# Decoder with a spiking delta-rule attention: chunk read on crossed quarters, sums of beta and alpha moved within the round

## The reference

```python
def step(carry, inp):
    s, mem = carry
    qt, kt, vt, sdt, abt, bbt = inp
    mem = DECAY * mem + sdt
    hard = (mem > THR).astype(x.dtype)          # the spike's value in the forward pass
    mem = mem - spike * THR
    alpha = jax.nn.sigmoid(abt + alpha_spike * spike)
    beta = jax.nn.sigmoid(bbt[..., None] + jnp.sum(spike * beta_spike, axis=-1, keepdims=True))
    active = (jnp.sum(hard, axis=-1, keepdims=True) > 0)
    alpha = jnp.where(active > 0, alpha, jnp.ones_like(alpha))
    beta = beta * active
    s = s * alpha[..., None]
    u = jnp.einsum('bhd,bhdv->bhv', kt, s)
    s = s - beta[..., None] * jnp.einsum('bhd,bhv->bhdv', kt, u)
    s = s + beta[..., None] * jnp.einsum('bhd,bhv->bhdv', kt, vt)
    out = jnp.einsum('bhdv,bhd->bhv', s, qt)
    return ((s, mem), out)
```

## Time and profile before

| | us |
|---|---|
| median of 3 runs | 1092.09 |
| lowest and highest | 1091.55, 1096.4 |
| profiled execution | 1096.75 |
| its span | 1095.0 |
| TensorE busy | 972.4 (89%) |
| VectorE busy | 698.6 (64%) |
| ScalarE busy | 482.7 (44%) |
| GpSimd busy | 208.7 (19%) |
| mean granted TensorE clock | 0.964 |

### The profile page before, as it was taken

One profiled execution on the slowest core, in us unless ns is written; L12 is line 12 of the kernel. 1 busy time (PEld: TensorE's weight loads), 2 busy tenths in 40 slices (PEclk: granted clock), 3 DMA queues, 4 the chain that ended last, 5 costly groups with the idle time before them and its releaser, 6 DMA issues. The chain is left out here.

```text
span 1095.0 us, 40049 instructions
## 1 busy us (share of the span) xinstructions
PE 972.4 (89%) x16722; PEld 648.9 (59%) x16722; DVE 698.6 (64%) x2514; ACT 482.7 (44%) x1378; POOL 208.7 (19%) x394
## 2 busy tenths in 40 slices
PE   7878768999998999999999888679999999999996
PEld 2333247777777777777777777446446546546542
DVE  2887886989889888898877765145424524714710
ACT  7667412555555555545555555313323423423311
POOL 7100201122122121221221220221210310310300
PEclk8999956999999999999999999889999999999999
DMA  3000000000000000000000000211000000100100
GB/s 97 0 1 1 1 1 3 4 4 4 4 4 4 4 4 4 4 4 4 4 5 11 22 4 4 96 37 27 7 1 21 24 1 15 27 1 3 31 1 10
DMA packets 18652, 13.83 MB, mean 13 GB/s; under 512 B 2491, under 2 KB 17259, under 8 KB 18475
## 3 DMA queue, kind: packets, MB, share of 16 engines
q1 hardware_dynamic: 18475, 11.28, 3.5%
HBM read 7.70 MB, written 1.05 MB: 8 GB/s over the span
## 5 line engine op out<-in xcount | busy, mean ns | idle before, releaser
L935 PE MATMUL banks<-work 64*64 64x64 f32 x3072 | 97.9, 234 | 24.9 <-DVE gates L674 12.9
L994 PE MATMUL banks<-work 64*64 64x32 f32 x2560 | 107.6, 224 | 5.8 <-ACT work L1351 5.0
L1285 ACT COPY work<-banks 128x128 f32<-128x128 f32 x160 | 42.8, 268 | 157.8 <-PE banks L970 157.7
L199 DVE SCALAR_TENSOR_TENSOR gates<-mom,gates 128x16 f32<-128x16 f32 x512 | 101.1, 197 | 9.5 <-ACT gates L1258 4.5
L203 DVE SCALAR_TENSOR_TENSOR mom<-gates 128x16 f32<-128x16 f32 x512 | 102.9, 201 | 5.0
L994 PEld LDWEIGHTS banks<-work 64*64 64x64 f32 x2560 | 92.5, 139 | 18.1 <-issue 10.0
L637 DVE COPY_PREDICATED gates<-work,banks 128x256 f32<-128x256 uint32 x192 | 101.9, 531 | 1.1
L935 PEld LDWEIGHTS banks<-work 64*64 64x64 f32 x3072 | 73.0, 139 | 43.2 <-issue 20.5
L531 POOL TENSOR_TENSOR mom<-mom 128x4 f32<-128x4 f32 x32 | 7.2, 223 | 384.4 <-ACT work L1330 384.4
L608 DVE TENSOR_TENSOR work<-work 128x256 f32<-128x256 f32 x160 | 67.8, 424 | 19.3 <-PE banks L935 18.7
L647 DVE TENSOR_TENSOR work<-work,banks 128x128 f32<-128x128 f32 x160 | 45.6, 285 | 48.4 <-PE banks L994 45.4
(11 more groups left out here) (263 smaller groups left out, 2140.8 us busy)
## 6 DMA issues: line engine op xcount, KB each, us to landing
work<-gates SPq DMA_DIRECT2D x28, 38.5 KB
qT<-in_x_dram SPq DMA_DIRECT2D x4, 256.0 KB, 3.8
work<-in_x_dram SPq DMA_DIRECT2D x4, 256.0 KB, 2.9
out_dram<-work SPq DMA_DIRECT2D x4, 256.0 KB, 2.3
gates<-in_w_ff_dram SPq DMA_DIRECT2D x3, 256.0 KB, 3.2
wv_sb<-in_wv_dram SPq DMA_DIRECT2D x1, 512.0 KB, 4.6
work<-in_w_out_dram SPq DMA_DIRECT2D x1, 512.0 KB, 4.0
gates<-in_x_Wq_dram SPq DMA_DIRECT2D x1, 512.0 KB, 5.0
```

The costliest lines, as they stand in the source:

```text
L199: ve.scalar_tensor_tensor(mem[:, :, t], neg_mem, -0.9, mem[:, :, t], ALU.mult, ALU.add).then_inc(charged, 1)
L935: last = pe.matmul(level_out(l)[to, a], KS[rows, n.two, hp], late[rows, hp], start=True, stop=True)
L994: last = pe.matmul(packed(psXT, l)[rows, a], Z[rows, l - 1, z], second_half(XT[:, n.two], l)[rows, a], start=True, stop=True)
L1285: ac.copy(first_half(Z[:, l - 1], l), packed(psZX_half, l)).then_inc(z_ok, 1)
```

## The change

The chunk read's outputs and the two halves of the state read swap partition halves (`to_out`), so that the chunk read uses crossed quarters; the tail's `front_out` reads the heads accordingly. The first three of the eight read products stand among the fifth XT products, the others at the round's end (`read_heads`, which has the three waits of `read_chunk` at each call). For gates from HP + 2 on (`early`), the alpha sums move from step 4 to step 2, `drive` from VectorE's step 4 to 2, and the sigmoid from ScalarE's step 5 to 3. The beta sums, their sigmoid and `beta` move from steps 1 and 2 of the following round to the end of the same round. The turn of KS moves from step 2 to 1. In step 4 of VectorE the query's scaling and two scan operations stand ahead of the add of XT. `prefixed` is the count of `kq_ok` for this: the last prefix counts one more where the next round's scaling precedes it.

```diff
--- before.py
+++ after.py
@@ -333,6 +333,9 @@
                 return by_chunk(counts(g))
             return counts(g).rearrange("p a (x t) -> p a x t", x=2)
 
+        def early(g):
+            return g.n > HP + 1
+
         def by_chunk_as(g, t):
             return t if g.n <= HP else t.rearrange("p (a x) t -> p a x t", x=2)
 
@@ -347,6 +350,9 @@
 
         def to_time(par, hp):
             return head_rows[hp // 2], 2 * par + hp % 2
+
+        def to_out(par, hp):
+            return head_rows[1 - hp // 2], 2 * par + hp % 2
 
         def at_level(par, hp):
             return head_rows[hp // 2], 2 * par + (hp // 2 + hp) % 2
@@ -381,6 +387,10 @@
 
         def by_chunk(t):
             return t.rearrange("p (b t) -> p b t", b=B)
+
+        def prefixed(n, l):
+            early = l == LEVELS - 1 and n.it + 1 < ROUNDS
+            return n.it * NKQ + l + 1 + early
 
         GATES = NC * HP
         QUARTER = C // HP
@@ -595,7 +605,7 @@
 
                 def prefix(n, l):
                     ve.wait_ge(lvl_mm, n.it * LEVELS + l + 1)
-                    ve.wait_ge(kq_ok, n.it * NKQ + l + 1)
+                    ve.wait_ge(kq_ok, prefixed(n, l))
                     if l == 0:
                         second = KQ[:, n.four].rearrange("p x a (j s) -> p x a j s", s=2)[:, :, :, :, 1]
                         by = aT[:, :, n.tok].rearrange("p a (j s) -> p a j s", s=2)[:, :, :, 0].unsqueeze(1)\
@@ -706,28 +716,33 @@
                         if l == 5 and gate:
                             alpha(gate)
                         spike(scan, h + 1)
+                        if l == 4 and aft2:
+                            scale_query(aft2)
+                        if l == 4:
+                            spike(scan, h + 2)
+                            spike(scan, h + 3)
                         if nxt:
                             add_xt(nxt, l)
-                        if l == 4 and gate:
+                        if gate and l == (2 if early(gate) else 4):
                             drive(gate)
-                        spike(scan, h + 2)
+                        spike(scan, h + (4 if l == 4 else 2))
                         if aft:
                             prefix(aft, l)
-                        spike(scan, h + 3)
+                        spike(scan, h + (5 if l == 4 else 3))
                         if aft:
                             suffix(aft, l)
-                        spike(scan, h + 4)
+                        if l != 4:
+                            spike(scan, h + 4)
                         if aft:
                             keep(aft, l)
-                        spike(scan, h + 5)
+                        if l != 4:
+                            spike(scan, h + 5)
                         if l == 1 and gate:
                             spikes(gate)
-                        if l == 2 and gate_old:
+                        if l == 2 and ramp == 0:
                             beta(gate_old)
                         if l == 3 and aft2:
                             scale_key(aft2)
-                        if l == 4 and aft2:
-                            scale_query(aft2)
                     spike(scan, 6 * NINV)
                     if cur:
                         update(cur, 0)
@@ -735,6 +750,8 @@
                     if aft2:
                         prefix(aft2, 0)
                         suffix(aft2, 0)
+                    if gate:
+                        beta(gate)
                     spike(scan, 6 * NINV + 1)
                     if aft2:
                         diagonal(aft2)
@@ -909,7 +926,7 @@
                 def level(n, l, gate=None, gate_old=None):
                     if l == 5 and gate:
                         pe.wait_ge(alpha_ok, gate.n + 1)
-                    if l == 3 and gate_old:
+                    if l == 1 and gate_old and gate_old.n >= HP:
                         pe.wait_ge(beta_ok, gate_old.n + 1)
                     if n.it == 0 and l == 0:
                         pe.wait_ge(zeroed, NZERO)
@@ -917,7 +934,7 @@
                         pe.wait_ge(folded, NFOLD)
                         pe.wait_ge(sd_ok, NSD)
                         pe.wait_ge(qk_ok, NQK)
-                    pe.wait_ge(kq_ok, n.it * NKQ + l + 1)
+                    pe.wait_ge(kq_ok, prefixed(n, l))
                     if l == 0:
                         pe.wait_ge(keys_ok, n.it + 1)
                     else:
@@ -981,19 +998,22 @@
                                          first_half(Z[:, l - 1], l)[rows, z], start=True, stop=True)
                     last.then_inc(x_mm, 1)
 
-                def make_xt(n, l, gate, gate_old):
+                def make_xt(n, l, gate, gate_old, cur=None):
                     if l == 1 and gate_old:
                         pe.wait_ge(be0_ok, gate_old.n + 1)
-                    if l == 5 and gate:
+                    if gate and l == (3 if early(gate) else 5):
                         pe.wait_ge(zal_ok, gate.n + 1)
                     pe.wait_ge(z_ok, n.it * NINV + l)
                     if n.it or l >= 2:
                         pe.wait_ge(xt_ok, n.it * NINV + l - 1)
-                    for head in straight:
+                    for i, head in enumerate(straight):
                         (rows, a), (_, z) = at_xt(*head), at_z(*head)
                         last = pe.matmul(packed(psXT, l)[rows, a], Z[rows, l - 1, z],
                                          second_half(XT[:, n.two], l)[rows, a], start=True, stop=True)
-                    last.then_inc(xt_mm, 1)
+                        if i == len(straight) - 1:
+                            last.then_inc(xt_mm, 1)
+                        elif l == NINV and cur and i % 2:
+                            read_heads(cur, halves[i // 2:i // 2 + 1])
 
                 def values(n):
                     pe.wait_ge(s_ok, n.it * 2)
@@ -1030,7 +1050,7 @@
                     for s in range(2):
                         for par in range(2):
                             hp = 2 * ((par + swap) % 2) + s
-                            (rows, hp), (to, a) = from_head(par, hp), to_time(par, hp)
+                            (rows, hp), (to, a) = from_head(par, hp), to_out(par, hp)
                             last = pe.matmul(o_out[to, a], KQ[rows, n.four, 1, hp], state[rows, n.b, hp, :],
                                              start=s == 0 and not swap, stop=False, skip_group_check=True)
                     last.then_inc(o_old if swap else o_half, 1)
@@ -1043,13 +1063,17 @@
                     pe.wait_ge(spk_ok, g.n + 1)
                     pe.matmul(counts(g), bdones[:, :], counts_as(g, spk[:, g.two]), start=True, stop=True).then_inc(count_mm, 1)
 
-                def spike_sums(g):
-                    pe.wait_ge(spk_ok, g.n + 1)
+                def spike_sums(g, nxt=None):
                     if g.n == 0:
                         pe.wait_ge(au_ok, NPAIR)
                         pe.wait_ge(padded, 2)
-                    if g.n:
-                        pe.wait_ge(beta_ok, g.n)
+                    if early(g):
+                        pe.wait_ge(be0_ok, g.n)
+                        pe.wait_ge(xt_ok, nxt.it * NINV + 1)
+                    else:
+                        pe.wait_ge(spk_ok, g.n + 1)
+                        if g.n:
+                            pe.wait_ge(beta_ok, g.n)
                     pe.matmul(psG[:, 0:B * C], wad_sb[:, g.hp, :], g.tokens(auT_all), start=True, stop=True)\
                         .then_inc(ab_mm, 1)
 
@@ -1064,15 +1088,16 @@
                     pe.matmul(psG[:, 0:B * C], bspike_bd[:, g.hp, :], spk[:, g.two],
                               start=False, stop=True, skip_group_check=True).then_inc(beta_mm, 1)
 
-                def read_chunk(n):
+                def read_heads(n, heads):
                     pe.wait_ge(e_ok, (n.it + 1) * LEVELS)
                     pe.wait_ge(o_old, n.it + 1)
                     pe.wait_ge(u_ok, n.it + 1)
-                    for head in halves:
-                        (rows, o), (_, a), (_, q) = to_time(*head), at_level(*head), at_x(*head)
-                        last = pe.matmul(o_out[rows, o], EA[rows, n.three, LEVELS, a], U[rows, q, :],
+                    for head in heads:
+                        (to, o), (rows, a), (_, q) = to_out(*head), at_level(*head), at_x(*head)
+                        last = pe.matmul(o_out[to, o], EA[rows, n.three, LEVELS, a], U[rows, q, :],
                                          start=False, stop=True, skip_group_check=True)
-                    last.then_inc(o_mm, 1)
+                    if heads[-1] == halves[-1]:
+                        last.then_inc(o_mm, 1)
 
                 def write_state(n):
                     pe.wait_ge(ksn_ok, n.it + 1)
@@ -1099,10 +1124,12 @@
                             spread_norm(3, l - 1)
                         if nxt:
                             make_z(nxt, l)
-                        if l == 1 and gate_old:
-                            beta_sums(gate_old, cur)
```

(40 more changed lines are left out.)

## The result

The changed kernel takes 1111.65 us (median of 4 runs, 1106.95 to 1117.86) against 1093.42 for the kernel before on the same chip: ratio 1.0144, 95% interval 1.0106 to 1.0183. Forecast were 1087.5 us and a range up to 1096; the time has the other sign and lies outside. The profiled execution took 1117.86 us (span 1116.1, before 1095.0).

A forecast was written before the change was run, and what follows sets the result against it. Neither TensorE (92% busy) nor VectorE (87%) was full, so their waits for each other bound the kernel. Gains 7.2+0.8+0.6 less losses 3.3 and 0.8 gave 4.5 us, taken off the 1092.09 median: about 1087.5, range 1077 to 1096.

The forecast's parts named there:

- Alpha sums in step 2: Sums on TensorE cost nothing under cover; drive replaces beta in VectorE's step 2, cost 0.06 us, level 3 at 10.08.
- Round's end: First state read's last product stays 0.85 us behind level 4, now 14.64; level 5 at 16.2, round 16.49 against 16.85.
- Step 4: Between levels 3 and 4, the alpha sums leave, 0.74 us less; level 4 at 13.78 us instead of 13.96.
- Beta at the round's end: Beta sums ahead of the read, and beta ahead of level 0's copy, put level 1 at 5.08 against 4.48: 0.60 lost.
- Read on crossed quarters: Fifth XT, held by the second state read and three inserted read products, ends 0.5 us later, bounds 0.2 to 0.9.
- rival 2: Slower: inserted read products hold the XT products behind them, 0.33 us in each of 30 rounds; time 1096, chance 0.11.
- VectorE's order in step 4: The query's scaling goes into VectorE's 0.80 us of idleness; alpha ends at 15.8 us instead of 16.51.
- Late rounds and the low clock: Rounds 25 to 30 lose 0.55 us each to held-up XT, 3.3 in all; low-clock rounds at the start gain 0.8 together.
- rounds -1 and 0: Two early rounds at low clock, TensorE nearly alone setting the pace: 0.8 us gained together for waits that go.
- slower: Outcome of a measured time above the 1097.6 us limit, about 0.5% over no change; chance 0.08.

The follow-up runs named there:

- e5: Changed kernel with GpSimd's keys and products held until keep 3 of the round before them, so they run in step 4: 1101.08 us, ratio 1.0044.
- e10: Kernel before, with only GpSimd's keys and products held until keep 3 of the round before them: 1096.03 us, ratio 1.0004.
- e4: Changed kernel with one swap on ScalarE in step 4, keep_out ahead of start_xt: 1103.42 us, ratio 1.0061.
- e2: Changed kernel with beta sums, their sigmoid, beta and the turn of KS back where the kernel before had them: 1102.84 us, ratio 1.0064.
- e1: Changed kernel with all eight read products behind the turn product, none among the fifth XT products, quarters still crossed: 1100.15 us, ratio 1.0038.
- e7: Changed kernel with the whole read as before: quarters uncrossed, all eight products behind the turn product: 1100.35 us, ratio 1.0007.
- e15: e9 with VectorE's order in step 4 as before too, so only alpha's move stays of the change: 1083.70 us, ratio 0.9861.
- e9: Changed kernel with the read and beta's work as before, keep_out ahead of start_xt and GpSimd's keys and products held until keep 3: 1073.78 us, ratio 0.9785.
- e6: Kernel before with the read's change alone: crossed quarters, three of eight products among the fifth XT products: 1103.97 us, ratio 1.0068.
- e3: Changed kernel with alpha sums, drive and alpha's sigmoid back in steps 4 and 5: 1128.82 us, ratio 1.0280.
- e14: Kernel before with alpha's move alone (sums and drive in step 2, sigmoid in step 3): 1093.68 us, ratio 0.9961.
- e13: Changed kernel entire, with keep_out ahead of start_xt and GpSimd's keys and products held until keep 3: 1094.57 us, ratio 0.9963.

## Why the prediction was wrong

In the round shown, level 5 came 0.72 us later than forecast (16.92 against 16.2): 0.33 up to level 3 (0.29 of it between levels 2 and 3), 0.31 between level 4 and the end of the first state read, 0.10 behind it, less 0.02 in step 4. Over 20 rounds that is 14.4 of the 21.2 us by which rounds 1 to 20 missed; the rest lies in rounds that were longer than the one shown, and is only in part explained.

- **Alpha sums in step 2: the step that failed.** It said that `drive` "replaces beta there ... cost 0.06", so that level 3 comes at 10.08; it came at 10.41 (median 10.44). I costed VectorE's operations at their usual length and counted only their number. The row of the collision stood in the timeline that the earlier trace rows are taken from, the charge of 0.71 at 421.43, and I passed over it; GpSimd's rows of that round I hadn't read. e5 puts the collision's price at 0.59 us a round in the changed kernel; some 0.24 of it the kernel before paid too (e10, to level 3), so that part was inside my rows.
- **Round's end: the second step that failed.** Step 4 was right in itself (level 3 to 4 3.68, forecast 3.70), but costed without the cover that it took away. With 0.74 us less on TensorE the round's end meets ScalarE's `keep_out`. The line "428.25 stands 0.85 behind level 4, so now 14.64" carried the distance over; it became 1.16 (the last product of the first state read), 0.31 more. e4 gives 0.24 back by one swap.
- **Beta at the round's end: right,** 0.60 forecast for level 1, 0.63 measured. The sum took it in as a loss, and e2 shows that it is one.
- **Read on crossed quarters: right in its size.** Level 5 came 1.67 behind the signal (the last product of the first state read, at 433.08), forecast 1.57; the inserted products step by 0.12 with XT instead of 0.06, so a third of rival 2 is true. That rival's rule (the Trainium skill, page "TensorE: Matmul & The Clock Gate", section "Part 3: Packing small matmuls — row/col tiling") is again not what the rows show: level 0's product at 419.57 (L947) starts ahead of the read's at 419.88 (L1097), which stands before it in the program. e1 shows that placing three products among XT costs 0.22 a scan round, which the forecast contained but didn't name as the thing to leave out; the swap of quarters by itself shows neither cost nor gain in the scan rounds (e7 against e1).
- **VectorE's order in step 4:** costed as filling idle time, worth 0.55 a round once alpha is what level 5 waits for (e15 against e9).
- **Late rounds and the low clock:** the forecast's 0.55 a round without gates isn't measured cleanly. In e6 rounds 25 and 26, without gates and at full clock like those before, took 17.13 and 16.03 instead of 15.89 and 15.29; in the changed kernel rounds 25 and 27 took 0.15 and 0.11 more than before. The changed kernel lost 6.9 us more than forecast there, beside 13.7 us more at the lower clock, half of which (6.9) would be lost if TensorE alone sets the pace, an estimate. The 4.8 us gained in rounds -1 and 0 go with 9.7 us less of it. No experiment tied either to an edit, and e3 warns that an edit can move the clock of every execution.
- **Rounds of 18 us.** Eight of the 20 scan rounds after the change took 17.7 to 18.2 us (before, the longest four took 17.3 to 17.5). Some hold a wait of TensorE for nothing that the profile shows:

```profile
360.71 0.59 PE L1011 MATMUL banks<-work 64*64 64x32 f32 x13 [0.86 <-issue]
```

  In the mean they make 0.2 us a round after the change (17.56 against the median 17.36), 0.1 before. Left open.

The sum by parts, from runs: alpha's move with both waits -0.4% (e14), without them -1.4% (e15); VectorE's order -0.8% (e9 against e15, where the intervals touch); beta and read together +1.8% (e13 against e9); the two waits +1.8% (the changed kernel against e13). The chances were wrong as well: slower had 0.08, and no rival ended above 1096, because none asked what the emptied steps would uncover.

## What to carry over

When work leaves a step, list every engine's last operation for that step and ask which is due next: here ScalarE's `keep_out`, 0.83 us behind a copy that nobody awaited. When an operation moves on VectorE, look at what GpSimd starts at that moment: a chain of small operations with two inputs in SBUF can lose 0.7 us to the wide operations beside it. Price the parts one at a time: one change held parts worth -1.4, -0.8 and +1.8%, and uncovered waits worth another +1.8%. And when a total agrees at last, compare it stretch by stretch: e13's does only because misses cancel.
